# The last scatters of a mixture of experts on two accumulators, read back interleaved and added on GpSimd and VectorE

## The reference

```
xn = layernorm(x)                                   # (16, 256, 128)
out = x + attention(xn) + ffn(xn)
# attention: q, k = elu(.)+1, S = k^T q, out = v S / sum(q*k), output projection,
#            y = xn + out, gamma * (y - mean) * rsqrt(var + eps) + beta
# ffn: shared_out = swiglu(xn, shared_w1, shared_w2)            384 hidden
#      gates = softmax(xn @ wg.T), the 8 largest of 64, made to sum to 1
#      each expert e (capacity 160): h = rows @ w1[e].T, y = (h1 * silu(h2)) @ w2[e].T
#      combined = zeros.at[token].add(y * gate);  ffn = shared_out + combined
```

## Time and profile before

| | us |
|---|---|
| median of 3 runs (range) | 367.81 (367.22 to 368.82) |
| the profiled execution | 367.13 |
| its span, first to last instruction | 365.3 |
| busy PE, DVE, POOL, ACT | 325.1, 279.4, 246.6, 196.2 |

### The profile page before, as it was taken

How to read it: one execution, slowest core, us unless ns; L and a number is a source line. 1 busy time by engine, 2 the same in 40 slices (tenths; PEclk the granted TensorE clock), 3 DMA queues, 4 the chain that set the end, 5 groups by cost and what they waited for, 6 DMA issues and landing times.

```text
span 365.3 us, 8486 instructions
## 1 busy us (share of the span) xinstructions
PE 325.1 (89%) x2765; PEld 307.3 (84%) x2765; DVE 279.4 (76%) x1083; ACT 196.2 (54%) x432; POOL 246.6 (67%) x205
## 2 busy tenths in 40 slices
PE   1799957789999999999999999999999999998910
PEld 0789956779999999999999999999998999998800
DVE  3888797868777868888787888888787878746384
ACT  3567727145747465665747465665737475643200
POOL 3142874355778788787878878788888777888210
PEclk9989988889999999999999999999999999999985
DMA  7999654921587878878886878778777878863859
GB/s 224 333 355 294 236 125 104 307 66 31 129 213 174 196 198 194 200 177 220 192 209 156 206 198 199 209 159 232 188 197 162 204 189 191 210 127 30 251 168 299
DMA packets 57739, 70.78 MB, mean 194 GB/s; under 512 B 12544, under 2 KB 45568, under 8 KB 57696
## 3 DMA queue, kind: packets, MB, share of 16 engines
q1 hardware_dynamic: 40032, 55.68, 50.1%
q0 software_dynamic: 15552, 13.51, 22.7%
q10 hardware_dynamic: 2112, 1.05, 1.0%
HBM read 54.78 MB, written 15.43 MB: 192 GB/s over the span
## 4 chain that ended last, share of the span: by engine, by line
PE 79%; DVE 6%; DMA 4%; issue 3%; ACT 3%; POOL 2%; SPq 1%; DVEq 0%; POOLq 0%
PE bank L1147 28%; PE bank L1157 11%; PE bank L1081 11%; PE bank L1090 5%; PE bank L1186 4%; PE bank L1166 3%; PE bank L1192 2%; DVE x_sb L1009 2%; PE bank L1044 2%; PE bank L1199 2%; DMA gath<-xng,idx_g 2%; DMA x_sb<-in_x 2%; PE bank L1207 2%; PE bank L1223 2%; PE bank L1121 1%
## 5 line engine op out<-in xcount | busy, mean ns | idle before, releaser
L446 POOL DMA_INDIRECT acc<-ys,idx_g x64 | 102.8, 1606 | 29.9 <-issue 15.5
L1147 PE MATMUL bank<-xe,ew 128*128 128x160 f32 x768 | 117.1, 302 | 1.0 <-ACT xe L554 0.6
L1147 PEld LDWEIGHTS bank<-xe,ew 128*128 128x128 f32 x768 | 108.3, 191 | 2.3 <-ACT xe L554 0.8
L427 POOL DMA_INDIRECT gath<-xng,idx_g x80 | 81.7, 1021 | 30.9 <-issue 22.6
L512 ACT ACTIVATE si<-bank 128x480 f32<-128x480 f32 (+1 forms) x96 | 52.0, 542 | 58.9 <-PE bank L1147 36.7
L685 DVE TENSOR_TENSOR ac<-si,bank 128x480 f32<-128x480 f32 x64 | 41.2, 644 | 19.6 <-ACT si L512 13.5
L1081 PE MATMUL bank<-xT,shw 128*128 128x128 f32 x384 | 53.8, 294 | 0.1
L1157 PE MATMUL bank<-ew,ac 128*128 128x128 f32 x384 | 53.4, 275 | 0.4 <-issue 0.4
L1157 PEld LDWEIGHTS bank<-ew,ac 128*128 128x128 f32 x384 | 49.5, 192 | 1.6 <-issue 0.8
L1081 PEld LDWEIGHTS bank<-xT,shw 128*128 128x128 f32 x384 | 49.9, 207 | 0.7 <-issue 0.4
L1090 PE MATMUL bank<-shw,acs 128*128 128x128 f32 x192 | 28.1, 283 | 8.2 <-DVE acs L676 5.8
(11 more groups left out here) (139 smaller groups left out, 558.5 us busy)
## 6 DMA issues: line engine op xcount, KB each, us to landing
ew<-in_expert_w SPq DMA_DIRECT2D x64, 384.0 KB, 3.5
ew<-in_expert_w SPq DMA_DIRECT2D x64, 192.0 KB, 3.3
ew<-acc SPq DMA_DIRECT2D x8, 512.0 KB, 5.2
x_sb<-in_x SPq DMA_DIRECT2D x8, 256.0 KB, 6.8
xng<-xn SPq DMA_DIRECT2D x8, 256.0 KB, 4.9
acc<-betas SPq DMA_DIRECT2D x4, 512.0 KB, 5.6
acc<-zeros SPq DMA_DIRECT2D x4, 512.0 KB, 4.9
gath<-xng,idx_g POOLq DMA_INDIRECT x80, 3.4
```

The source lines that it names most:

```text
L427: pool.indirect_dma_start(out=gath[:, p, m, :], out_offset=None, in_=xng, in_offset=bass.IndirectOffsetOnAxis(ap=idx_g[:, g % 4, m:m + 1], ...
L446: pool.indirect_dma_start(out=acc[adds_to[g, m]], out_offset=bass.IndirectOffsetOnAxis(ap=idx, axis=0), in_=src, in_offset=None, compute_o ...
L1147: last = pe.matmul(h_view(n, half_ + 1, CAP)[:, c, :], ew[p][m][:, k * P:(k + 1) * P], xe[:, p, m, :], start=True, stop=True)
```

## The change

Three things change. The table alternates to its end, so `(15, 3)` goes to `acc[0]`, and `(15, M)` waits for `(15, 2)` and no longer for `(15, 3)`. SP waits for `acc[0]`, issues its first two reads, waits for `acc[1]`, and issues the other six in turn from both. The eight adds of `acc[0]` move from VectorE to GpSimd, behind its last scatter; VectorE keeps those of `acc[1]`, each waiting for GpSimd's add of that step (`sum_done`).

```diff
--- before.py
+++ after.py
@@ -66,8 +66,7 @@
     for g in range(1, NG):
         scatters += [(g - 1, 2), (g - 1, 3), (g, 0), (g - 1, M), (g, 1)]
     scatters += [(NG - 1, 2), (NG - 1, 3), (NG - 1, M)]
-    flip = scatters.index((NG - 1, 1))
-    adds_to = {u: 1 if n > flip else (n + flip) % 2 for n, u in enumerate(scatters)}
+    adds_to = {u: n % 2 for n, u in enumerate(scatters)}
 
     QUAD = 4
 
@@ -342,16 +341,26 @@
                 sp.wait_ge(y_full, down_at['e', g, 2] + 1)
                 down_weights(g + 1, 3)
 
-            def acc_load(k):
+            def acc_landed(k):
+
                 sp.wait_ge(a_full, a_at['rest', NG - 2 + k] + 1)
                 for g, m in [u for u in scatters if adds_to[u] == k][-M - 1:]:
                     sp.wait_ge(s_sc[m], 16 * (g + 1))
-                for h in range(M):
-                    n = slice(NA * h, NA * h + NA)
-                    sp.dma_start(ew[k][h][:, 0:NA * D].rearrange("p (n d) -> p n d", d=D), acc_n[k][:, n, :]).then_inc(acc_in[k][h], 16)
-
-            acc_load(0)
-            acc_load(1)
+
+            def acc_load(k, h):
+                n = slice(NA * h, NA * h + NA)
+                sp.dma_start(ew[k][h][:, 0:NA * D].rearrange("p (n d) -> p n d", d=D), acc_n[k][:, n, :]).then_inc(acc_in[k][h], 16)
+
+            acc_landed(0)
+            acc_load(0, 0)
+            acc_load(0, 1)
+            acc_landed(1)
+            acc_load(1, 0)
+            acc_load(0, 2)
+            acc_load(1, 1)
+            acc_load(0, 3)
+            acc_load(1, 2)
+            acc_load(1, 3)
             for r in range(0, NR, 2):
                 sp.wait_ge(fin_done, r + 1)
                 sp.dma_start(out_n[:, tiles(r), :], x_sb[:, tiles(r), :]).then_inc(out_sem, 16)
@@ -477,6 +486,11 @@
                 scatter(g, 1)
             for m in (2, 3, M):
                 scatter(NG - 1, m)
+
+            for r in range(NR):
+                pool.wait_ge(acc_in[0][RB * r // NA], 16)
+                pool.wait_ge(res_done, RB * (r + 1))
+                pool.tensor_tensor(x_sb[:, tiles(r), :], x_sb[:, tiles(r), :], acc_back(0, r), ALU.add).then_inc(sum_done, 1)
 
         @block.scalar
         def _(act):
@@ -997,16 +1011,11 @@
                 shared_add(EARLY + g)
                 if a < B:
                     attention_stats(a)
-
-            def add_back(k, r, step):
-
-                if r % 2 == 0:
-                    dve.wait_ge(acc_in[k][r // 2], 16)
-                if k == 1:
-                    dve.wait_ge(sum_done, r + 1)
-                else:
-                    dve.wait_ge(res_done, RB * (r + 1))
-                dve.tensor_tensor(x_sb[:, tiles(r), :], x_sb[:, tiles(r), :], acc_back(k, r), ALU.add).then_inc(step, 1)
+            def add_back(r):
+
+                dve.wait_ge(acc_in[1][RB * r // NA], 16)
+                dve.wait_ge(sum_done, r + 1)
+                dve.tensor_tensor(x_sb[:, tiles(r), :], x_sb[:, tiles(r), :], acc_back(1, r), ALU.add).then_inc(fin_done, 1)
 
             finish(B - 3)
             shared_mul(NT - 4)
@@ -1019,9 +1028,8 @@
             shared_mul(NT - 1)
             shared_add(NT - 1)
             finish(B - 1)
-            for k, step in ((0, sum_done), (1, fin_done)):
-                for r in range(NR):
-                    add_back(k, r, step)
+            for r in range(NR):
+                add_back(r)
 
         @block.tensor
         def _(pe):
```

## The result

The changed kernel takes 370.94 us (median of 10 runs, 369.7 to 372.6) against 368.25 for the kernel before in the same session (10 runs, 367.22 to 369.47). The ratio is 1.0065 [1.0046, 1.0084]: slower, and clear of noise. The median lies outside the range given. The profiled execution took 369.7 us with a span of 367.8, before 367.13 with 365.3.

A forecast was written before the change was run, and what follows sets the result against it. The end was taken as held by writes queued behind acc[1]'s reads, with VectorE's adds close behind; earlier reads against engines taking turns put the last write at 365.0 against 364.9, +0.1 us, median 367.9, range 365.0 to 369.6.

The forecast's parts named there:

- The scatters: Last two scatters on GpSimd: (15, 3) begins at 339.3 in place of 341.4, (15, M) at 341.4 in place of 347.3.
- For (15, M) I take 4.1: Last scatter: 4.1 us from its start to SP's third read, issued at 345.5, 5.2 us earlier than before.
- no landing is waited for in this: GpSimd's and VectorE's final adds: data always there in time, add 4 at 350.5 for 352.3, add 6 at 353.1 for 355.3.
- rival 3: (15, M) caught behind the first two reads (5.9 us), GpSimd's adds 4 and 6 wait: +0.5, 368.3 median; chance 0.10.
- Each further one 1.27 us behind: SP's eight reads: the first lands at 346.7, each further one 1.27 us later, the last at 355.6.
- The adds: At the end GpSimd and VectorE take turns: 1.12 us per GpSimd add, 0.55 per VectorE add; last add ends at 361.7.
- Rival 2: GpSimd keeps the port while it has adds, finish(B - 1) runs only behind add 6: +1.5 us, 369.3 median; chance 0.13.
- The sum: Whole kernel: last write lands at 365.0 against 364.9, +0.1 us on the profiled 367.13; median 367.9.
- This is the whole gain: Reads at the end are out of the way 3 us sooner, which is the gain if the adds can follow.

The follow-up runs named there:

- e3: The kernel before with only the table of accumulators changed, so (15, 3) adds to acc[0]; old read order, all adds on VectorE: 369.01 us, ratio 1.0003.
- f2: The kernel before with acc[0]'s adds on GpSimd, each also waiting for GpSimd's add before it to complete: 367.16 us, where the kernel before takes 364.54.
- j1: The kernel with the changed table and VectorE adding in order of landing, rerun unchanged on another chip: 362.52 us against 364.1, ratio 0.9965.
- j3: The kernel before, no edit, a fourth trace on the chip of j1: 366.39 us in one execution.
- e2: The changed kernel with reads in the old order, four of acc[0], then the wait, then four of acc[1]; GpSimd still adds acc[0]: 369.24 us, ratio 1.0010.
- e1: The changed kernel with all sixteen adds back on VectorE, acc[0] first; table and interleaved reads stay changed: 371.86 us, ratio 1.0060 to the kernel before.
- e4: The kernel before with only the adds of acc[0] moved to GpSimd; table and reads as before: 372.55 us, ratio 1.0090.
- the chip of i: One chip's runs without an edit: the kernel before twice, 369.98 and 371.54 us, and the changed kernel once, 372.92 us.
- i1: The kernel before, no edit, run again for a second trace: 369.98 us against 370.35, ratio 0.9997.
- i2: The kernel before, no edit, run again on the same chip for a third trace: 371.54 us in one execution.
- g1: e3 with VectorE adding in the order in which the reads land, instead of all acc[0] first: 362.58 us, ratio 0.9940 to the kernel before.

## Why the prediction was wrong

**The scatters: starts right.** (15, 3) started at 340.47 and (15, M) at 342.96, in a trace whose mark is 1.9 us later; set back by that, 338.6 and 341.05 against 339.3 and 341.4. Both wait for their sources alone.

**"For (15, M) I take 4.1", and with it "no landing is waited for in this": the steps that failed.** From (15, M) to SP's third read it took 5.1, 6.0 and 6.4 us in the three traces of the changed kernel (342.96 to 348.04; 343.68 to 349.64; -8.06 to -1.64 from the mark). In e3, with four reads ahead, it took 6.0 as well (-8.05 to -2.05). The bound of 5.9 was on the table as rival 3, with a chance of 0.10; it was the likely case, and GpSimd's adds 4 and 6 waited for data as it said. The amount of data is not what decides: the row with 4.1 had 2 MB of reads behind its scatter, the changed kernel has 1 MB. What goes with the times in these traces is how soon the first read is issued behind the scatter's start. After 1.4 to 1.5 us it took 3.7 to 4.1 (four scatters: the first trace, f2, j1, j3), after 0.75 to 1.3 us it took 5.1 to 6.4 (twelve scatters, those of the changed kernel at 0.8 to 0.9). The forecast of 1.3 us was at the edge of that. Why it is so stays open.

What I left out is what stood behind the wait. In the old order a late scatter holds back only parts of `acc[1]`, which VectorE doesn't begin to add before 6.2 us behind the mark. In the new one it holds back parts 2 and 3 of `acc[0]`, which the very next adds need. The forecast had part 2 landed 1.4 us behind the mark. It landed at 4.9, 3.0 and 3.9, and in e2 and e3 at 1.3 and 1.2. GpSimd stood 2.98 us for it in the profiled trace, and VectorE 2.63 for part 1 of `acc[1]`, the next in the queue.

**"Each further one 1.27 us behind": right only in a full queue.** The third read was issued 0.6, 1.5 and 2.0 us later than forecast, while part 2 landed 3.5, 1.6 and 2.5 us late. So in the profiled trace most of the lateness, 2.9 us, is slow steps between landings and not the scatter. The usual step is 1.22 to 1.34. The others are 1.4 to 4.2, most of them at the start of a batch and around the blocked wait, and in the profiled trace of the changed kernel only one of seven steps is the usual one. The forecast had the last read 6.5 behind the mark; it landed at 10.8, 9.2 and 10.7, and even in order (e2, e3) at 8.0 and 8.1. What makes these steps long is not shown.

**The adds: right in mechanism and price.** In the changed kernel the small instructions of finish(B - 1) take 0.63, 1.34, 0.35 and 0.35 us, the last two while GpSimd stands for data; VectorE's adds run up to 1.75, GpSimd's up to 1.75. In e2, with data there, all four take 1.1 to 1.3. The Trainium skill (Perfetto Trace Analysis, Optimizing Scalar/DVE Operations) says that moving work between these engines might not help. The traces agree: e3 to e2 is +0.07%, e1 to the changed kernel +0.05%, both within the intervals. Rival 2's shut-out didn't happen in the changed kernel and did in e4.

**The base: one trace of a kernel that has two kinds of end.** The sum was made against one trace, whose end of 16.2 us is of the long kind. The end forecast for the changed kernel, 365.0 + 0.4 - 349.1 = 16.3, is near what its three traces have on average (16.8, 15.5, 16.9: 16.4). That is luck: the last read was 2.7 to 4.3 us later than forecast, yet VectorE's last add ended 13.1, 11.8 and 12.2 behind the mark against 12.6. I read that as fewer turns between two engines that stand for data; no run separates the two errors. On the chip of i the kernel before ends 15.2 behind the mark twice and the changed one 16.9 once; in the first session it is 16.2 and 16.8. The larger difference, 1.7 us, would be most of the losses measured on two other chips, 2.7 and 1.9 us (370.94 less 368.25; 370.57 less 368.7). What makes up the rest no trace shows.

**"This is the whole gain": none where it was measured.** I gave the earlier scatters a gain by earlier reads and said that the adds decide whether it arrives. e3 shows the table alone at 1.0003, on a chip where the traces have a late mark. There the last write was held by the adds of VectorE (issued at 11.12 behind the mark in e3, as in the first trace, i1 and i2), and the reads of `acc[1]` were through by 8.1, as in i2. In the traces with an early mark the late reads do hold the writes: the last one lands at 15.8 and 16.6, against 14.8 in e3. So on such a chip the table alone could gain 1 to 1.8 us; it wasn't run there, and it is a rival to the order of the adds as the source of g1's gain.

**The rest of the difference, and what stays open.** The profiled pair has 0.6 us of its 2.5 us behind the mark and 1.9 ahead of it. Of these 1.9 us nothing comes from an instruction that the change touches. The sixth last of VectorE's 32 adds of a shared product stands 1.9 us apart already (before, then changed), 16 us ahead of the first scatter that the two kernels treat differently:

```profile
322.55 0.29 DVE L691 TENSOR_TENSOR x_sb<-x_sb,bank 128x128 f32<-128x128 f32 x1 [0.26 <-PE bank L1090]
```

```profile
324.45 0.29 DVE L705 TENSOR_TENSOR x_sb<-x_sb,bank 128x128 f32<-128x128 f32 x1 [0.26 <-issue]
```

Why GpSimd keeps VectorE out in e4 and not in e2 isn't settled: in e4 its first add begins beside the end of the scatter before it (349.15 against 348.14 + 1.55 = 349.69) and each next one begins 0.6 us before the last one's shown end; f2 breaks this up and the turns come back.

## What to carry to other kernels

Before a wait is moved ahead in a queue, list what stands behind it and when each is needed; then price the wait by the longest row that resembles it. A chain of scatters made shorter is worth nothing where the consumer's own order holds the output back, so find out first which of the two does. And take the end of a kernel from several traces before summing against it: here it differed by 1.8 us between traces of the same code, where the change was forecast at 0.1 and measured at 2.7.

## What the runs showed of the hardware that was not expected

- A scatter that adds to HBM took 3.2 to 3.5 us from its start to its landing, or to the instruction that waited for it, without reads. With 1 to 2 MB of reads issued 0.75 to 1.3 us behind its start it took 5.1 to 6.4, with 1.4 to 1.5 us only 3.7 to 4.1. With 2 MB issued ahead of it, it took 5.9 to 8.2 where they began 2.1 to 2.6 us before (first trace, j3, f2), and 4.1 to 4.6 where they began 4.6 to 5.6 before (i1, i2, e4).
- GpSimd can shut VectorE out for 6.7 us over several instructions (e4), though in e2 they alternate, a small instruction of VectorE and an add of GpSimd in 1.27 us. The Trainium skill (SBUF — State Buffer, SBUF: two separate sides) has the shared pair of ports held for one whole instruction, by whoever starts first. e2 agrees with that (1.1 to 1.35 us per small instruction). e4 does not. Nor does f2 in one place: VectorE's instruction began 0.55 us before GpSimd's first add is shown to begin, and ended behind it, 2.56 us later. In e4 the adds are shown 1.85 us long and stand 1.22 apart. The Trainium skill (Perfetto Trace Analysis, GPSIMD Engine Instruction) advises to time GpSimd's instructions by their spacing, and by that the trace agrees: the work itself is the 1.22 to 1.27 us seen elsewhere.
- Identical code (the kernel before, four traces on three sessions' chips) reaches the same point near the end at 347.5 to 354.6 us; two traces on one chip differed by 2.0.
